# Weights of later phases fetched in chunks by SyncE during the low-head attention phases of a two-layer decoder

## What is computed

```
x = LN(x + self_attention(x))                 # 16 heads of 8
x = LN(x + causal_cross_attention(x, ctx))    # 16 heads of 8
x = LN(x + ternary_feed_forward(x))           # 128 -> 512 -> 128, plus a low-rank path
x = LN(x + differential_attention(x))         # 16 heads of 64, two softmaxes
x = LN(x + latent_attention(ctx, x, mask))    # 16 heads of 64
x = LN(x + mixture_of_experts(x))             # 8 experts, 128 -> 512 -> 128
```

## Time and profile before

| | us |
|---|---|
| runs shown, median (lowest to highest of 3) | 1827.52 (1826.65 to 1832.11) |
| the profiled execution, its own time | 1828.64 |
| its span, first to last instruction | 1826.9 |
| PE busy | 1648.0 (90%) |
| DVE busy | 1192.0 (65%) |
| ACT busy | 904.5 (50%) |
| POOL busy | 670.0 (37%) |

### The profile page before, as it was taken

The page is one execution under the profiler, slowest core; times in us unless marked ns, Lnnn a source line. Parts: engine busy times, 40 slices in busy tenths (PEclk is TensorE's granted clock), DMA queues, the critical chain, the costliest instruction groups (busy, mean ns, idle before and its releaser), DMA issues. The chain is left out here.

```text
span 1826.9 us, 51823 instructions
## 1 busy us (share of the span) xinstructions
PE 1648.0 (90%) x18030; PEld 1356.5 (74%) x18030; DVE 1192.0 (65%) x3409; ACT 904.5 (50%) x2614; POOL 670.0 (37%) x1071
## 2 busy tenths in 40 slices
PE   6998599958789999999999999599999999999585
PEld 4776377747767777777777777489999999999454
DVE  4777376756657776776677677446777777777444
ACT  3666266634334545444454544155565665656131
POOL 2555155431113333333333333123444444444235
PEclk9999699979999999999999999889999999999798
DMA  1111411101110001001100100221111111111231
GB/s 47 41 39 38 154 48 46 51 19 55 42 31 25 24 26 31 23 23 30 27 23 27 31 23 23 58 56 52 57 56 56 56 51 47 52 56 54 58 90 53
DMA packets 156933, 82.27 MB, mean 45 GB/s; under 512 B 17562, under 2 KB 154060, under 8 KB 156465
## 3 DMA queue, kind: packets, MB, share of 16 engines
q1 hardware_dynamic: 149728, 71.35, 14.1%
q10 hardware_dynamic: 5072, 6.66, 1.1%
q0 software_dynamic: 2048, 3.15, 0.5%
HBM read 61.03 MB, written 21.27 MB: 45 GB/s over the span
## 5 line engine op out<-in xcount | busy, mean ns | idle before, releaser
L1122 PE MATMUL bank<-diff_xT,diff_w_score 128*128 128x128 f32 x2048 | 259.8, 281 | 0.8 <-ACT diff_xT L1226 0.8
L1122 PEld LDWEIGHTS bank<-diff_xT,diff_w_score 128*128 128x128 f32 x2048 | 242.4, 193 | 22.4 <-issue 20.6
L1233 ACT ACTIVATE diff_keys<-bank 128x512 f32<-128x512 f32 x256 | 152.4, 595 | 166.2 <-PE bank L1122 166.2
L1889 POOL TENSOR_TENSOR lat_prob<-lat_prob,lat_inv_sum 128x512 f32<-128x512 f32 x128 | 133.6, 1044 | 226.2 <-DVE lat_inv_sum L1803 209.8
L1416 POOL TENSOR_TENSOR diff_prob<-diff_prob,diff_inv_sum 128x512 f32<-128x512 f32 x64 | 67.2, 1050 | 380.6 <-DVE diff_inv_sum L1320 380.6
L1705 ACT ACTIVATE lat_prob<-bank,lat_neg_max 128x128 f32<-128x128 f32 x512 | 180.5, 372 | 1.0 <-DVE lat_neg_max L1825 1.0
L1716 ACT ACTIVATE lat_query<-bank 128x512 f32<-128x512 f32 x128 | 76.5, 597 | 172.9 <-PE bank L1601 172.9
L1631 PE MATMUL bank<-lat_catT,lat_query 128*128 128x128 f32 x1024 | 143.6, 284 | 3.9 <-ACT lat_query L1716 3.9
L1601 PE MATMUL bank<-lat_catT,lat_w_score 128*128 128x128 f32 x1024 | 138.8, 280 | 1.3 <-DVE lat_mask_bias L1863 0.9
L1631 PEld LDWEIGHTS bank<-lat_catT,lat_query 128*128 128x128 f32 x1024 | 126.8, 195 | 6.4 <-ACT lat_query L1716 5.4
L1601 PEld LDWEIGHTS bank<-lat_catT,lat_w_score 128*128 128x128 f32 x1024 | 127.8, 196 | 3.2 <-issue 1.2
(11 more groups left out here) (306 smaller groups left out, 3671.1 us busy)
## 6 DMA issues: line engine op xcount, KB each, us to landing
lat_c_rep<-cat SPq DMA_DIRECT2D x128, 128.0 KB
diff_x_rep<-stage SPq DMA_DIRECT2D x128, 32.0 KB
lat_c_t<-cat SPq DMA_DIRECT2D x32, 128.0 KB, 2.1
exp_w<-in_L_ffn_w_dram SPq DMA_DIRECT2D x16, 256.0 KB
expert_rows<-lat_zeros SPq DMA_DIRECT2D x4, 548.0 KB
exp_rows<-expert_rows SPq DMA_DIRECT2D x8, 274.0 KB, 5.2
self_x_t<-in_x_dram SPq DMA_DIRECT2D x32, 64.0 KB
self_x_res<-in_x_dram SPq DMA_DIRECT2D x32, 64.0 KB, 1.9
```

What stands on the lines that cost most here:

```text
L1122: last = nc.tensor.matmul(ring[(k + d) % 2][:, j * P:(j + 1) * P], w_score[:, H1 * (k // 2) + HS * d + 4 * (k % 2) + j, :], xT[:, :], star ...
L1233: nc.scalar.activation(keys[:, k // 2, 4 * (k % 2):4 * (k % 2) + 4, :].rearrange("p h t -> p (h t)"), ring[(k + d) % 2][:, :], ACT.Copy).t ...
L1889: nc.gpsimd.tensor_tensor(prob[:, q, :, :], prob[:, q, :, :], inv_sum[:, q, :, None].to_broadcast([P, 4, T]), ALU.mult)\
```

## The change

`transfers()` of a set of weights now returns the list of its transfers (tile, source, semaphore). The two low-head phases flatten the lists of all their `early` sets into one list `later`. The scalar block issues none of them any more. SP issues them in slots 1 to 7: in slot i the entries i-1, i+6, i+13, ... of the list, between its load of `x_res` and its store of a result. Wq, Wk and Wv of the two later attentions are cut into chunks of 512 columns (2 KB a row, 256 KB a chunk), so that four (or two) transfers raise one semaphore, and the waits on these semaphores go from 16 to `early.all`, 64 or 32. Wo stays one transfer of 512 KB.

So `self` issues its 11 transfers as 2, 2, 2, 2, 1, 1, 1 in slots 1 to 7. `cross` now has 20 transfers, 3 in each of slots 1 to 6 and 2 in slot 7. Both transfers of Wo fall in slot 6, with one chunk.

```diff
 class EarlyLoads:
+    def transfers(self):
+
+        return [(tile, source, self.loaded) for tile, source in self.parts]
+
     def start(self, eng):
-        for tile, source in self.parts:
-            eng.dma_start(tile, source).then_inc(self.loaded, 16)
+        for tile, source, loaded in self.transfers():
+            eng.dma_start(tile, source).then_inc(loaded, 16)
...
+        later = [transfer for weights in early for transfer in weights.transfers()]
         block = ctx.enter_context(nc.Block())
...
                     sp.dma_start(x_res[:, par, :], x_in[bass.ds(i, 1), :, :].rearrange("o p d -> p (o d)"))\
                         .then_inc(res_loaded[par], 16)
+                if isinstance(i, int) and 1 <= i < 8:
+                    for tile, source, loaded in later[i - 1::7]:
+                        sp.dma_start(tile, source).then_inc(loaded, 16)
                 if here(on, i, -3):
...
-            for weights in early:
-                weights.start(act)
             slots(act, slot)
...
-    def start(self, eng):
-
-        for n, w in enumerate(self.sources[:3]):
-            eng.dma_start(self.raw[:, n, :, :].rearrange("p t d -> p (t d)"), w).then_inc(self.loaded[n], 16)
-        eng.dma_start(self.wo[:, :, :], self.sources[3].rearrange("(t p) d -> p t d", p=P)).then_inc(self.wo_loaded, 16)
+        self.chunks = pairs_of_heads // 4
+        self.all = 16 * self.chunks
+
+    def transfers(self):
+
+
+        parts = [(self.raw[:, n, 4 * c:4 * c + 4, :].rearrange("p t d -> p (t d)"), w[:, 4 * P * c:4 * P * (c + 1)],
+                  self.loaded[n]) for n, w in enumerate(self.sources[:3]) for c in range(self.chunks)]
+        return parts + [(self.wo[:, :, :], self.sources[3].rearrange("(t p) d -> p t d", p=P), self.wo_loaded)]
...
-                pe.wait_ge(loaded[n], 16)
+                pe.wait_ge(loaded[n], early.all)
```

More of the change, by code:

```diff
@@ L974, in _ @@
             dve.wait_ge(lam_done, 3)
-            dve.wait_ge(loaded[2], 16)
+            dve.wait_ge(loaded[2], early.all)
             nc.vector.tensor_scalar(wv2[:, :, :], raw[:, 2, NT // 2:NT, :], vo_scale[:, :], None, ALU.mult)\
@@ L1213, in pair @@
                         last.then_inc(wo_done, 1)
-            pe.wait_ge(early.loaded[2], 16)
+            pe.wait_ge(early.loaded[2], early.all)
             pe.wait_ge(early.wo_loaded, 16)
```

## The result

| | before | after |
|---|---|---|
| first comparison, median (lowest to highest) | 1827.24 (1826.52 to 1832.11), 5 runs | 1817.03 (1814.28 to 1821.23), 5 runs |
| ratio, 95% interval | | 0.9947 [0.9928, 0.9965] |
| profiled execution, its own time | 1828.64 | 1821.23 |
| its span | 1826.9 | 1819.5 |

Over all 17 runs of the changed kernel the median is 1820.4, from 1814.1 to 1823.3.

What follows compares the result with a forecast made beforehand. PE, busy 90% of the span, bounds the kernel, so moved transfers matter only where it stands still. Gains of 4.15 + 6.0 = 10.15 us gave 1818.5 from the profiled 1828.64, 1817.4 from the median; forecast 1817.5, range 1814.5 to 1822.5.

Steps and rivals of the forecast that it cites:

- Self, 4.15 us: Start of self: without ACT's 11 issues the first copy comes at 9.85 instead of 14.00, gaining 4.15 us.
- Cross start, 6.0 us: Start of cross: without ACT's 8 issues and their traffic the first copy comes at 199.95, not 205.97; gain 6.0 us.
- The sum, 10.15: Gains at the two phase starts together: 4.15 + 6.0 = 10.15 us less, with the added work on SP costing 0.
- cost 0, up to 2 us if slot 6 goes worse: SP's DMA queue in cross: chunks and Wo ahead of the next inputs cost 0, at worst up to 2 us.
- the sign that I had named for being wrong: In cross, PE waiting at L288 in slots 2 to 8 would mean stalled issues or late inputs.
- the arrival of the input at 8.8 us after SP's store: Slot 6 of cross: next inputs there by 245.7, wanted by PE at 247.6, leaving 1.9 us.
- Rival (a), the clock: At cross's start PE's clock rise keeps its moment, taking back 2.5 to 5 us; time 1820 to 1822.5; chance 0.10.
- Rival (b), stalls of the issue: SP's issues in cross slots stall 5.48 us each; over seven slots 7 us, time about 1824.5; chance 0.07.
- Rival (c): One phase start doesn't gain, likelier the first load of cross; sum then 5.75, time 1821.8; chance 0.08.
- Rival (d): Cross inputs come late behind chunks in one queue; at 90 GB/s 17.9 us more, time 1835.4; chance 0.03.

Runs made afterwards that it cites:

- pool_start: Changed kernel, but the 8 whole transfers of cross are issued at the phase's start by GpSimd; 0.9942 of the kernel before, median 1818.01.
- burst_act: Changed kernel, but ACT issues the 8 whole transfers of cross at the end of its slot 0; 0.9985 of the kernel before, median 1823.24.
- self_only: Kernel before with the change in self alone; in cross ACT still issues its 8 whole transfers at the start; ratio 0.9969, median 1820.88.
- wo_first: Changed kernel with both Wo at the head of their lists, so no slot has both; run twice, 0.9939 of the kernel before each time, medians 1816.78 and 1815.06.
- whole: Changed kernel without cutting into chunks, 8 whole transfers in slots 1 to 7 of cross; 0.9937 of the kernel before, median 1817.56.
- rows4k: Changed kernel with each Wo read as 128 rows of 4 KB instead of 1024 of 512 bytes, leaving Wo permuted; 1814.33 in one run.

## Why the prediction was right, and where it was not

**Self, 4.15 us: right.** 14.00 to 9.63 is 4.37; the table load waits for nothing. The end of self then gains 4.7 to 5.6 us where the clock rises early.

**Cross start, 6.0 us: right.** 8.77 to 2.79 is 5.98, 4.36 of it from the load (6.45 to 2.09) and the rest from ACT's queue, as the sum had them. Of the two causes, the price of the traffic was shown on its own by `pool_start` (context loads landing 5.4 and 10.6 us after their issue with ACT's queue free, though not the first one), and that of the busy ACT queue by `burst_act`; `self_only` has both again.

**The sum, 10.15: right for the mechanism, and reached where slot 6 is mended.** In `wo_first`, `wo_first2` and `whole` cross item 31 comes 10.3 us earlier than before (362.65, 362.58, 362.63 against 372.93). In the changed kernel's second and third profiles it is 7.7 and 7.6, in the first, with the late clock in self, 5.1. The parts are not those of the sum, though. In the three profiles with 10.3 self gives 5.2 to 5.5 of it and cross 4.8 to 5.2, mainly because the tail of self (from item 31 to the weight preparation of cross) takes 23.2 to 23.6 us there and 22.6 before.

That the first median came within 0.5 us of the forecast is luck. The wait and the low clock of slot 6 were not in the sum, the pooled median is 2.9 us above the forecast, and in the first profile the phases that no edit touched gave back 2.3 us of what was missing.

**Slot 6, "cost 0, up to 2 us if slot 6 goes worse": mis-sized.** This is also the sign that I had named for being wrong: PE waits for an input in slots 2 to 8. The step that failed is the arrival of the input at 8.8 us after SP's store (245.7 in the slot shown, with the store at 236.89), which left 1.9 us of room. Measured it was used at 246.4 with the store at 234.72, 11.7 us. Two terms make the 2.9 us. The second Wo landed 9.7 us after the store where I had its data moved after 8.2: some 0.45 of these 1.5 us is the slow issue (1.06) ahead of the chunks. The rest stays open; short rows explain little of it, as in `rows4k` it landed 9.5 us after the store. And the input was used 2.0 us behind it, where I had given it 0.6, as I counted the moving of 128 KB there and not its landing: 1.4 us. And the price of a wait of 1 us wasn't 1 us but 2.65, since the clock fell behind it. That is more than the 2 us that the term allowed.

**Rival (a), the clock: it came in 3 of the 14 profiles, but not as told.** The rise moves with the start, in cross too (at 206 us, 7.6 after the first projection at 198.44), and in self one of the two profiles with the old start has it late as well. **Rival (b), stalls of the issue: right not to count on it.** The chunks took 0.4 to 1.6 us in cross, and single issues in self up to 2.05. The fifth transfer stalled in every kernel that issued Wq, Wk, Wv and Wo back to back from ACT or from SP (3.93 to 5.48 us), and not from GpSimd (0.57). It isn't the number of rows: slot 6 issued over 2000 of them in 0.43, 0.43 and 0.58 us. **Rival (c)** is refuted by the 2.09 us of the first load, and that load reads the context, which no phase writes. (The slices of the earlier trace rows are not all full from the fifth on, the last five fall from 291 to 0; nothing rests on it.) **Rival (d)** was the right mechanism at a small size: one wait of 1 us, in the slot with the least room, while the other slots have none.

**The version with the shorter cross phase** is the changed kernel with Wo at the head of each list, 0.9939 in both comparisons, or without the chunks, 0.9937. That either is faster in whole runs than the changed kernel is not shown.

## What to carry to other kernels

Prefetches at the start of a phase cost twice: the queue that issues them stands before the first useful instruction, and their traffic stands before the first input. Moving them behind the first slots, on a queue with nothing to do there, gave back 4.4 and 6.0 us. When they are spread, spread the bytes evenly over the slots, and check the fullest slot with the landing time of the next input (2 us here), not with its transfer time. A wait of 1 us on TensorE can cost 2.7 when its clock falls behind it, as in slot 7 in five profiles of five, though a wait of 1.18 us early in the phase did not bring it down. So the last fraction of a microsecond of room can be worth more than it seems.

## What was not expected of the hardware

- The stall of the fifth transfer: 2.1 to 2.5 us after the first issue and behind 3.5 MB, it took 3.9 to 5.5 us from SP's or ACT's queue; 3 MB were issued ahead of the fourth, which took 0.66 to 1.04. From GpSimd's queue, behind the same 3.5 MB and 2.8 us after the first issue, it took 0.57.
- PE's wait of 1.0 to 1.3 us in slot 7 was followed by the lower clock in all five profiles that had it (steps of 6.91 to 6.98 behind it), and one of 0.27 us was not. Nor was the wait of 1.0 to 1.2 us for POOL right after the rise in cross, in eleven profiles. So its length alone doesn't decide, and what does isn't shown. In `pool_start` the wait of 3.25 us was followed by it too.
- 512 KB in rows of 512 bytes landed 5.1 and 6.3 us after the issue, and in rows of 4 KB hardly sooner, 5.2 and 6.0.
- Single issues of SP in the slots written out took 1.0 to 2.1 us instead of 0.43, before the change as after it, for no reason that the profile shows.
